# Where the layer norms' epsilon is added: on GpSimd, or on VectorE directly behind mean and variance

## The reference, cut to what matters

```python
def _layernorm(x, axis=-1, eps=1e-05):
    m = jnp.mean(x, axis=axis, keepdims=True)
    v = jnp.var(x, axis=axis, keepdims=True)
    return (x - m) / jnp.sqrt(v + eps)
...
x = x + jnp.tanh(g_xattn[0]) * _L0_xattn_ref(_layernorm(x, axis=-1), ctx_1024, ctx_1024, ...)
x = x + jnp.tanh(g_ffn[0]) * _L0_ffn_ref(_layernorm(x, axis=-1), ...)
x = x + jnp.tanh(g_xattn[1]) * _L1_xattn_ref(_layernorm(x, axis=-1), ctx_1024, ctx_1024)
x = x + jnp.tanh(g_ffn[1]) * _L1_ffn_ref(_layernorm(x, axis=-1), ...)
```

## Time and profile before

| | us |
|---|---|
| median of 3 runs | 164.79 |
| lowest, highest | 164.42, 164.83 |
| the profiled execution | 164.3 |
| its span, first to last instruction | 162.6 |
| TensorE busy (share of the span) | 134.2 (83%) |
| VectorE busy | 105.1 (65%) |
| ScalarE busy | 93.4 (57%) |
| GpSimd busy | 88.2 (54%) |
| L351, the additions of epsilon on GpSimd, 24 | 5.7 |
| L355, the powers, 24 | 14.9 |
| share of TensorE in the chain that ended last | 48% |
| share of GpSimd, of VectorE in it | 18%, 10% |

### The profile page before, as it was taken

The page is one execution under the profiler, slowest core; times in us unless marked ns, Lnnn a source line. Parts: engine busy times, 40 slices in busy tenths (PEclk is TensorE's granted clock), DMA queues, the critical chain, the costliest instruction groups (busy, mean ns, idle before and its releaser), DMA issues.

```text
span 162.6 us, 4195 instructions
## 1 busy us (share of the span) xinstructions
PE 134.2 (83%) x1438; PEld 100.8 (62%) x1438; DVE 105.1 (65%) x359; ACT 93.4 (57%) x234; POOL 88.2 (54%) x200
## 2 busy tenths in 40 slices
PE   0799999999999899899886865968289729999990
PEld 0796977676858567474554534845144218998990
DVE  2455992995669798989996896684148416223344
ACT  0172439527483867868896977956354863666000
POOL 2489969608173664737887587377754500355400
PEclk9999999999999999999999997585557995999998
DMA  5950130401900048002920000000000040000143
GB/s 119 297 213 4 10 125 4 133 26 16 359 27 0 0 143 371 14 0 60 387 83 0 0 0 2 0 6 16 16 29 14 21 130 0 20 23 26 32 129 131
DMA packets 6117, 12.15 MB, mean 75 GB/s; under 512 B 876, under 2 KB 4360, under 8 KB 5840
## 3 DMA queue, kind: packets, MB, share of 16 engines
q1 hardware_dynamic: 5008, 10.33, 18.8%
q0 software_dynamic: 512, 0.76, 1.5%
q10 hardware_dynamic: 576, 0.79, 1.3%
HBM read 9.47 MB, written 2.63 MB: 74 GB/s over the span
## 4 chain that ended last, share of the span: by engine, by line
PE 48%; POOL 18%; DVE 10%; issue 9%; DMA 9%; ACT 3%; POOLq 0%; ACTq 0%; DVEq 0%; SPq 0%
POOL rs L355 6%; PE bank L930 6%; PE bank L1170 5%; PE bank L974 5%; PE bank L993 5%; PE bank L947 4%; PE bank L970 4%; PE bank L1181 4%; PE bank L1008 4%; POOL disp_dram L389 3%; DMA wk<-wk_in 2%; POOL ve L351 2%; POOL pr L340 2%; PE bank L1064 2%; DMA disp<-disp_dram 2%
## 5 line engine op out<-in xcount | busy, mean ns | idle before, releaser
L340 POOL TENSOR_SCALAR_AFFINE_SELECT pr<-pr 128x512 f32<-128x512 f32 x32 | 20.2, 647 | 14.2 <-ACT pr L464 14.1
L679 DVE TENSOR_REDUCE nmax<-bank 128x4 f32<-128x512 f32 x32 | 20.1, 683 | 2.8 <-PE bank L974 2.6
L464 ACT ACTIVATE pr<-bank 128x512 f32<-128x512 f32 x32 | 18.1, 597 | 6.6 <-PE bank L993 6.5
L409 POOL DMA_INDIRECT moe_dram<-zeros,tok_i x8 | 7.8, 970 | 16.7 <-DVE zeros L885 15.5
L355 POOL TENSOR_TENSOR rs<-ve,half_neg 128x1 f32<-128x1 f32 (+1 forms) x24 | 14.9, 622 | 2.0
L930 PE MATMUL bank<-ctx_t,wk 128*128 128x128 f32 x64 | 11.1, 335 | 5.2 <-DMA wk<-wk_in 5.2
L1008 PE MATMUL bank<-pr,v_st 128*32 128x128 f32 x256 | 12.8, 283 | 1.5 <-POOL pr L340 1.4
L596 ACT ACTIVATE h_t<-bank,cols 128x128 f32<-128x128 f32 x32 | 9.1, 368 | 8.1 <-PE bank L1170 8.1
L930 PEld LDWEIGHTS bank<-ctx_t,wk 128*128 128x128 f32 x64 | 10.2, 244 | 5.3 <-DMA wk<-wk_in 5.2
L389 POOL DMA_INDIRECT disp_dram<-z_tok,put_i x8 | 8.2, 1021 | 6.3 <-DVE put_i L823 3.6
L974 PEld LDWEIGHTS bank<-k,q 9*128 9x128 f32 x256 | 7.9, 186 | 3.4 <-issue 3.4
(11 more groups left out here) (174 smaller groups left out, 349.7 us busy)
## 6 DMA issues: line engine op xcount, KB each, us to landing
iw<-iw_in SPq DMA_DIRECT2D x1, 2048.0 KB, 9.1
ow<-ow_in SPq DMA_DIRECT2D x1, 2048.0 KB, 7.8
w_raw<-w_ffn_in SPq DMA_DIRECT2D x1, 768.0 KB, 7.8
rows<-rows_in SPq DMA_DIRECT2D x1, 576.0 KB, 4.9
disp_dram<-zeros SPq DMA_DIRECT2D x1, 516.0 KB, 4.7
disp<-disp_dram SPq DMA_DIRECT2D x2, 258.0 KB, 2.9
ctx_tok<-ctx_tok_in SPq DMA_DIRECT2D x1, 512.0 KB, 3.5
w_res<-w_res_in SPq DMA_DIRECT2D x1, 512.0 KB, 3.9
```

The costliest lines, as they stand in the source:

```text
L340: g.affine_select(out=pr[:, n % NPR, :, :], in_=pr[:, n % NPR, :, :], compare_op=ALU.is_ge, fill=0.0, base=0, pattern=[[0, HU], [1, P]], c ...
L464: act.activation(pr[:, n % NPR, :, :], unit_bank("scores_t", u, b)[:, :].rearrange("p (j q) -> p j q", j=HU), ACT.Exp, scale=float(DK) ** ...
L679: v.tensor_reduce(nmax[:, b % 2, HU * u:HU * u + HU], unit_bank("scores", u, b)[:, :].rearrange("p (j k) -> p j k", j=HU), AX.X, ALU.max, ...
```

## The change

The addition of epsilon moves from GpSimd's `rstd` to VectorE's `aggr`. There it stands directly behind the aggregation and waits for its result; the semaphore that tells GpSimd (and, for k = 0, VectorE's own `center_f`) that mean and variance are there is now incremented by the addition. GpSimd's step begins with the power for k = 0 and 1, and with L353 for k = 2. The first norm's addition (L295) stays where it was. The tables of orders are the same. A line number behind this place is one less on GpSimd and two more in VectorE's later steps in the changed kernel.

```diff
--- before.py
+++ after.py
@@ -348,7 +348,6 @@
                     m, v_ = mv[:, k, b], ve[:, k, b]
                     n = 2 if k == 2 else 1
                     g.wait_ge(s[var_sem], b + 1)
-                    then(g.tensor_scalar(v_[:, 0:1], m[:, 1:2], EPS, None, ALU.add))
                     if k == 2:
                         then(g.tensor_scalar(v_[:, 1:2], v_[:, 0:1], EPS_IN, m[:, 1:2], ALU.mult,
                                              ALU.add))
@@ -714,7 +713,10 @@
             def aggr(k, var_sem):
                 def step(b):
                     needs((k, "stats", b))
-                    v.bn_aggr(mv[:, k, b, :], st[:, k, b, :]).then_inc(s[var_sem], 1)
+                    mark((k, "aggr", b), v.bn_aggr(mv[:, k, b, :], st[:, k, b, :]))
+                    needs((k, "aggr", b))
+                    v.tensor_scalar(ve[:, k, b, 0:1], mv[:, k, b, 1:2], EPS, None,
+                                    ALU.add).then_inc(s[var_sem], 1)
                 return step
 
             def center_f(b):
```

## The result

| | before | after |
|---|---|---|
| median, us | 164.81 | 162.36 |
| lowest, highest | 164.42, 165.08 (4 runs) | 161.79, 164.08 (4 runs) |
| ratio, 95% interval | | 0.9871 (0.9832 to 0.9910) |
| the profiled execution | 164.3 | 162.66 |
| its span | 162.6 | 160.9 |

The change makes the kernel 2.1 us faster (1.5 to 2.8). A second set of runs says the same: 0.9856 (0.9828 to 0.9884); of its six executions one (164.20) fell in a slower state of the chip and is left out of the ratio. Forecast were 1.2 us, 163.6, with a range of 162.5 to 165.4: the direction was right and the size is nearly twice as large.

The account below looks back on a forecast made before the run. TensorE bounds to about 75 us, then the layer norms on VectorE and GpSimd. Gains of 0.3 to the residual, 0.2 to the scatter and 0.7 behind it make 1.2 us: 163.6 us, range 162.5 to 165.4.

Parts of the forecast that it names:

- Its price of an addition: VectorE's queue, each of 24 added additions: 0.19 us, between ends of 0.12 and 0.30, in all 4.6 us.
- Up to about 74 us: nothing: Stretch to about 74 us: TensorE holds the chain, VectorE's waits cover the additions, so no gain.
- the isolated norm's gain: One norm alone, from the aggregation's end to the power: 0.24 us instead of 0.40, a gain of 0.16 us.
- Gain at 87.79: 0.0: VectorE's step at 87.79: the 1.18 us wait for GpSimd goes, but VectorE's own queue ends at 87.75, gain 0.0.
- The gate step stays, the residual gains 0.3: VectorE's gate step at 99.53 keeps its time as six additions fill its wait; the residual at 104.60 comes 0.3 earlier.
- The scatter 0.5 earlier: Scatter at 111.26: starts 0.5 us earlier, 0.3 from the residual and 0.2 behind it; the indices stay at 110.01.
- The last two norms 0.34 each: Two norms behind the scatters, inputs ready on GpSimd: two additions removed, 0.34 us each, 0.68 in all.
- Rival 1: VectorE binds harder, 0.25 to 0.30 us an addition: 0.3 faster to 0.3 slower, 164.5 to 165.1 us; chance 0.19.
- Rival 4: VectorE's additions lengthen GpSimd's instructions by some 0.07 us each: gain only 0.6, 164.2 us; chance 0.10.
- rival 2: TensorE's clock stays low in 106.8 to 110.4 us, up to 2.3 us more work: 0.6 slower, 165.4; chance 0.14.
- Rival 3: TensorE's low clock phase near 100 us doesn't begin: 0.7 more, gain 1.9, 162.9 us; chance 0.12.
- The tail is fixed, 45.05: From the last ScalarE pass at 117.55 to the end: stays 45.05 us, so the end gains what that pass gains.

Follow-up runs that it names:

- the early eighteen: Against the kernel before, 18 early additions moved to VectorE, the six of k = 1 from block 6 and k = 2 from block 4 left on GpSimd: 163.71 us.
- the late six: Against the kernel before, only the additions of k = 1, blocks 6 and 7, and k = 2, blocks 4 to 7, moved to VectorE: 163.75 us.
- the last two: Against the kernel before, only the additions of k = 2, blocks 6 and 7, moved to VectorE: 163.11 us, ratio 0.9918.
- the folded one: Against the changed kernel, 20 VectorE additions replaced by a constant third group in the aggregation, inner 1e-12 left out: 159.68 us.
- the probe: Against the kernel before, the aggregation reads a third group adding 0.5 to the variance, and GpSimd adds epsilon minus 0.5: 165.02 us, one run.

## Why the prediction was right in direction and too small

**Its price of an addition: right.** 153 ns where 0.12 to 0.15 stood; the centring follows 0.40 us behind the aggregation's start (77.87 to 78.27) where it was 0.21 before: 0.19. An instruction that doesn't wait for the addition follows 0.28 to 0.29 us behind the aggregation, as forecast (0.28 to 0.30); for the centring, which waits for it, the 0.40 was not. The removal of all additions confirms the price: 0.93 us for five and 1.21 for six. The prediction had drawn from the Trainium skill's "VectorE: DVE Perf Modes", section "The DRAIN you can't avoid", that the added instruction would cost only itself. That is not borne out: 0.153 us of duration cost 0.19 us of queue. The prediction's objection to the section was only half right, though: the same section of the Trainium skill says, too, that a next instruction that is not held starts earlier, and with that L764's 0.09 us agrees.

**"Up to about 74 us: nothing": wrong by 0.12.** One norm of the second attention lay on the path there. The chain of waits before, then after, at that place (start, us, what):

```profile
64.58 0.30 DVE st L711
...
65.49 0.58 POOL rs L355
...
66.15 0.27 POOL nmr L366
66.42 0.60 POOL pr L340
```

```profile
63.91 0.31 DVE st L710
...
64.69 0.58 POOL rs L354
...
65.36 0.26 POOL nmr L365
65.62 0.59 POOL pr L340
```

The power starts 0.91 us behind the statistics before and 0.78 after, and the mask behind it (L340) is what TensorE waits for. The 0.13 is the isolated norm's gain, forecast at 0.16. The chain showed L340 behind a power, and I had looked for it only from 74 us on.

**"Gain at 87.79: 0.0": this step failed, 0.46 was measured** (0.12 of it from further ahead). The stall did go, and VectorE's own queue was next, as said. But it came sooner than worked out. From the gate step to `step_f:6` the changed kernel takes 13.60 us (73.05 to 86.65), the kernel before took 13.94 with its wait. The gain from here on is 0.34, and it has two pieces. One of the six additions cost nothing: before, `x2` started 0.30 us behind the aggregation (81.43 to 81.73), and 0.29 behind it now (81.05 to 81.34), with the addition in between; so five of them lengthen the path and not six (measured 0.93: 12.67 us from 73.85 to 86.52 before, 13.60 now; forecast 1.14). And VectorE could have gone on 0.21 us behind the start of the step in front, as it now does (86.44 to 86.65), not at its end, which lies 0.08 later: the ready time before was 86.52, not 86.61. 86.52 + 0.93 = 87.45 against 87.79: 0.34. The kernel without additions takes the same 12.67 us over this stretch, which confirms the new ready time. The test of the step stands in two traces: the early eighteen alone give 0.47 there, the late six 0.00.

**"The gate step stays, the residual gains 0.3": the same error carried on.** At `gate_t:7`, 0.58, and at `x3:4`, 0.62. The prediction had VectorE without a gain at 87.79, and then let six additions fill the wait of 1.15 us at the gate step (98.38 + 1.14 = 99.52). The first half was off by 0.46. In the second half the six additions made the stretch from `step_f:6` to `gate_t:7` 1.03 us longer (10.59 without the wait, 11.62 now), because waits inside it gave some back: 0.46 + 1.15 - 1.03 = 0.58. That VectorE itself sets the gate step was right. (97.97 + 0.95 is 98.92 and not 98.95; nothing hangs on it.) GpSimd's scale of 98.21, said to come 0.46 earlier, came 1.19 earlier from zero, and the sigmoid was over at 97.63 when VectorE reached the gate step at 98.27. GpSimd and ScalarE in the changed kernel:

```profile
96.34 0.30 POOL L372 TENSOR_SCALAR fa<-w_step,fa 128x1 f32<-128x1 f32 x1
...
96.96 0.67 ACT L518 ACTIVATE sg<-bank,fa 128x512 f32<-128x512 f32 x1
```

So of the two rounding passes behind it, the first (99.40) came 0.95 us earlier, where 0.4 stood, and the second (102.14) 0.59, where it was said to stay. In the changed kernel TensorE starts its four transposes 0.06 us behind the end of the second, so the residual hangs on it and gained 0.62 with it.

**"The scatter 0.5 earlier": 0.85.** 0.62 up to `x3:4`, and 0.23 behind it, where 0.2 stood (the late six alone give 0.22, the second trace of the changed kernel 0.10). The size of this term was right, but partly by luck. The prediction had the indices stay at 110.01 and the scatter gain 0.5 even so; since the scatter needs 0.89 us behind the indices, it would then have gained 0.36. The indices came 0.61 earlier from zero, with VectorE's queue.

**"The last two norms 0.34 each": 0.82 for both.** The mechanism was right, the size off by 0.14: it had been read from one start to the next, without the longer hand-over in front (0.38 and 0.44 us). Why the hand-over was longer stays open, as said.

**The rivals.** Rival 1, VectorE binding harder, fell with the price of 0.19. But its direction was nearer to the truth than the main line: VectorE's additions take back 2.3 of 3.97 us. Rival 4, interference, did not come. The power on one column took 592 ns, before 570, on two columns 711, before 726; but it took 589 and 714 in the kernel without any addition, and 572 and 727 where both engines add, so VectorE's additions are not what moved it. By the Trainium skill's "SBUF — State Buffer", in its section on the two separate sides, the two engines lock each other out in VectorE's two-port modes; no row here shows such a hold, and none shows which mode the addition takes. Rivals 2 and 3 had the clock's phases change. In the first trace of the changed kernel they came along with the work, 1.2 GHz in 98.8 to 105.2 us and 2.4 in 106 to 108, as in the earlier trace rows a little earlier. In the second, rival 2's condition did come about: the clock stayed low in 106.4 to 108.4 (0.50). Its price did not. Against the first trace the residual of block 7 came 0.49 us later, not 2.3; the last variance still lay ready in front of GpSimd; and the last pass came only 0.14 later, through the indices, which the lower clock held back by 0.24. Rival 3 showed in no trace.

**"The tail is fixed, 45.05": wrong as a premise.** It was read from one execution, and that one was the shortest of twelve (45.05 to 46.73). The time ahead of zero is chance in the same way. In the pair of profiles the two chances nearly cancel (0.68 won, 0.65 lost), so that the difference of spans, 1.7 us, is by luck that at the last pass, 1.67.

**What stays open.** The steps give 1.53 to 1.67 us up to the last pass, and the runs 2.1 to 2.4. The same surplus stands in the early eighteen (0.66 by steps, 1.1 by medians), the last two (0.75 and 1.5) and the kernel without additions (3.97 and 4.8), and not in the late six (1.03 and 1.0) or where both engines add (slower by 1.18 and 1.1). A hint is the mean granted clock of whole executions: it is at 0.909 of the full one or more in 12 of 59 runs of the kernel before, in 7 of 10 of the changed kernel, in all five of the folded one, in 7 of 10 of the early eighteen, 4 of 6 of the last two and 4 of 5 of the kernel without additions; in 2 of 8 of the late six and in none of the eight where both add. In the changed kernel those with the higher clock took 162.16 us (median), the others 162.65, 164.08 and 164.20. In the kernel before the two kinds hardly differ, 164.57 and 164.72. Perhaps an earlier routing leaves TensorE at 1.2 GHz less often in the stretch where the experts begin. The kept traces don't show it: behind the last pass the early eighteen took 46.3 us and the last two 46.1, the kernel before 45.05 and 46.48. No run here sets that clock, so where these 0.4 to 0.9 us come from is not shown.

## What to carry to other kernels

A small addition moved between two engines is worth what it frees on the one minus what it takes on the other, at each place where one of them ends last; here 3.97 minus 2.3 us. A form in which nobody adds (a constant group in the aggregation's input) brought the residual 2.93 us forward, as much as leaving epsilon out (2.92). Where a stall goes and the engine's own queue is next, the new ready time decides the sum: take it from the cadence of start to start, and strike each added instruction that lies ahead of another wait. Compare two traces from an event behind the chances of the start up to the last event that repeats, and check on a second profile of the same kernel which stretches repeat: two traces of the kernel before agreed within 0.02 us at six steps over 82 us and differed by 0.7 and 1.4 us outside. Look at the granted clock of both before you read a difference as the change's: 0.14 us in the changed kernel and 0.3 us in the probe were the clock's.

## What the runs showed of the hardware

- VectorE's aggregation takes a third group of count zero and adds its third value, divided by the count of all, to the variance: 194 ns instead of 180.
- A 128x1 addition costs GpSimd's queue 0.38 to 0.44 us where inputs lie ready, and VectorE's 0.19 to 0.20, at durations of 238 and 153 ns.
- TensorE's granted clock went up for the first time at 11.16 us in one execution of the kernel before and at 9.20 in another; eight products of 128x128 there took 1.92 and 1.06 us, and the later steps keep 0.7 us of that shift.
- An indirect scatter on GpSimd started 0.69 us behind the end of GpSimd's instruction in front of it or 0.89 behind the end of the indices' last instruction on VectorE, whichever was later, in twelve of twelve traces.
